# A gather loop on GpSimd written out, with constant waits and its indices loaded 256 columns at a time

## The reference

```python
h = (x_flat @ W_gat).reshape(M, HEADS, NUM_EXPERTS)     # 4 heads, 4 experts
loops = jnp.arange(M); src = concat([edge_index[0], loops]); dst = concat([edge_index[1], loops])
a_src = (h * att_src).sum(-1);  a_dst = (h * att_dst).sum(-1)
e = leaky_relu(a_src[src] + a_dst[dst], negative_slope=0.2)
e_max = segment_max(e, dst);  ee = exp(e - e_max[dst])
denom = segment_sum(ee, dst);  alpha = ee / (denom[dst] + 1e-16)
agg = segment_sum(h[src] * alpha[:, :, None], dst) + b_gat
scores = layernorm(agg).mean over heads;  top-2 of 4 experts, softmax weights
out = sum over experts of gate * (gelu(x @ W1 + b1) @ W2 + b2)
```

## Time and profile before

| | us |
|---|---|
| median of 3 runs | 11243.61 |
| lowest and highest | 11234.59 and 11244.57 |
| span of the profiled execution | 11633.8 |
| POOL busy in it | 7643.2 (66%) |
| DVE busy in it | 7098.4 (61%) |
| PE busy in it | 6698.5 (58%) |
| ACT busy in it | 4807.1 (41%) |

### The profile page before, as it was taken

The page is one execution under the profiler, slowest core; times in us unless marked ns, Lnnn a source line. Parts: engine busy times, 40 slices in busy tenths (PEclk is TensorE's granted clock), DMA queues, the critical chain, the costliest instruction groups (busy, mean ns, idle before and its releaser), DMA issues. The chain is left out here.

```text
span 11633.8 us, 85668 instructions
## 1 busy us (share of the span) xinstructions
PE 6698.5 (58%) x21383; PEld 2861.9 (25%) x21383; DVE 7098.4 (61%) x5424; ACT 4807.1 (41%) x5351; POOL 7643.2 (66%) x4827
## 2 busy tenths in 40 slices
PE   0178888888888888888859699700000000000569
PEld 0133333333333333333323233300000000000432
DVE  8689999999999999999953377611111111111334
ACT  0066666666666666666623277511111111110124
POOL 0089999999999999999963300076666666665027
PEclk8599999999999999999988699855555555555569
DMA  0166666666666676666640000032222222220012
GB/s 9 31 158 180 179 178 178 177 178 181 176 179 178 177 180 174 180 179 179 177 109 1 9 1 1 3 37 16 17 16 17 16 17 16 17 16 9 3 52 89
DMA packets 422049, 1072.84 MB, mean 92 GB/s; under 512 B 130450, under 2 KB 165906, under 8 KB 419554
## 3 DMA queue, kind: packets, MB, share of 16 engines
q1 hardware_dynamic: 336898, 1043.89, 34.4%
q0 software_dynamic: 75808, 26.27, 5.2%
q10 hardware_dynamic: 9216, 1.05, 0.1%
HBM read 1005.93 MB, written 63.50 MB: 92 GB/s over the span
## 5 line engine op out<-in xcount | busy, mean ns | idle before, releaser
L535 POOL TENSOR_TENSOR hC<-h,Cb 128x1024 f32<-128x1024 f32 x1536 | 3601.4, 2358 | 434.1 <-DVE h L630 410.6
L630 DVE TENSOR_TENSOR_SCAN h<-dA,B_ps 128x1024 f32<-128x1024 f32 x1344 | 3073.2, 2287 | 156.4
L308 PE MATMUL y_ps<-hC,con 128*128 128x512 f32 x6144 | 2965.9, 605 | 81.9 <-DVE gz L636 80.3
L2583 POOL DMA_INDIRECT g_got<-scratch_node,g_idx x2048 | 1946.2, 950 | 904.2 <-issue 904.0
L455 ACT ACTIVATE dA<-delta,negA 128x1024 f32<-128x1024 f32 x1344 | 1535.1, 1145 | 1202.1 <-DVE h L630 1200.2
L616 DVE TENSOR_TENSOR B_ps<-dx,B_ps 128x1024 f32<-128x1024 f32 x1344 | 1623.1, 1208 | 166.2 <-PE B_ps L302 166.2
L2599 PE MATMUL g_ps_y<-g_wout,g_hid 128*128 128x64 f32 x512 | 125.8, 427 | 2546.2 <-issue 1541.7
L308 PEld LDWEIGHTS y_ps<-hC,con 128*128 128x128 f32 x6144 | 1184.2, 193 | 1145.4 <-issue 940.9
L2669 DVE TENSOR_TENSOR g_e<-g_tgt,g_got 128x128 f32<-128x128 f32 x64 | 27.1, 424 | 2059.5 <-DMA g_got<-scratch_node,g_idx 2059.5
L302 PE MATMUL B_ps<-Bpart,sel 96*128 96x512 bf16 x2688 | 827.6, 390 | 651.1 <-DVE h L630 649.0
L2623 ACT ACTIVATE g_w_ps<-g_w 128x128 f32<-128x128 f32 x64 | 18.0, 281 | 2238.8 <-DVE g_m L2677 935.3
(11 more groups left out here) (475 smaller groups left out, 10879.8 us busy)
## 6 DMA issues: line engine op xcount, KB each, us to landing
Cb<-scratch_c_rows SPq DMA_DIRECT2D x3072, 256.0 KB, 4.0
drive<-scratch_c_rows SPq DMA_DIRECT2D x384, 256.0 KB, 5.1
g_got<-scratch_node,g_idx POOLq DMA_INDIRECT x2048
eb_share<-scratch_gate_rows SPq DMA_DIRECT2D x128, 256.0 KB, 3.5
scratch_c_rows<-BCrow SPq DMA_DIRECT2D x96, 256.0 KB, 4.0
scratch_edge<-g_out SPq DMA_DIRECT2D x64, 384.0 KB
par<-in_ssm SPq DMA_DIRECT2D x48, 395.5 KB, 5.1
scratch_place<-s_zero SPq DMA_DIRECT2D x4, 1024.0 KB, 10.6
```

The costliest lines, as they stand in the source:

```text
L308: last = nc.tensor.matmul(y_ps[:, hs], con[:, K_ID:K_ID + P], hC[k % DEEP][:, hs], start=(k == 0), stop=(k == STEPS - 1))
L535: G.tensor_tensor(hC[k % DEEP][:, :], hst[k % DEEP][:, :], Cb[k % DEEP][:, :], ALU.mult).then_inc(prod_ready, 1)
L630: V.tensor_tensor_scan(hst[k % DEEP][:, ::step], decayed[:, ::step], driven[:, ::step], 0.0, ALU.mult, ALU.add).then_inc(scanned, 1)
L2583: nc.gpsimd.indirect_dma_start(out=got[k][:, j, :], out_offset=None, in_=node_tbl, in_offset=Off(ap=idx[k][:, j:j + 1], axis=0)).then_inc( ...
```

## The change

POOL's loop is replaced by a program written out over all 64 chunks. The addition on `gate` and the semaphore `opened` go. At the head of each chunk POOL waits on `consumed` against a constant, and at every eighth chunk on the load of the indices. The index tiles become two tiles of 256 columns, each for eight chunks (`SPELL`); SP loads them, two ahead of everything else and the other six between its stores, and SP's loop over pairs is written out as well. ACT's wait on `consumed` and its index load go.

```diff
-            gate, spare = sb("gate", [P, GOTS + 1]), sb("spare", [P, 4])
-            idx = [sb(f"idx{k}", [P, CHUNK], i32) for k in range(GOTS)]
+            spare = sb("spare", [P, 4])
+            SPELL = 8
+            idx = [sb(f"idx{k}", [P, SPELL * CHUNK], i32) for k in range(2)]
...
 (SP)
-                    for k in range(GOTS):
-                        sp.dma_start(idx[k][:, :], x["src"][:, k * CHUNK:(k + 1) * CHUNK]).then_inc(idx_here[k], 16)
+                    def load_idx(b):
+                        sp.dma_start(idx[b % 2][:, :], x["src"][:, b * SPELL * CHUNK:(b + 1) * SPELL * CHUNK]).then_inc(idx_here[b % 2], 16)
+
+                    for b in range(2):
+                        load_idx(b)
...
-                    with sp.Fori(0, CHUNKS // 2) as pair:
-                        for k in range(2):
-                            c = pair * 2 + k
-                            sp.wait_ge(copied_out, c * 2 + 4)
-                            sp.dma_start(edge_v[:, bass.ds(c * (CHUNK * ROW_O), CHUNK * ROW_O)],
-                                         out[k][:, :, :].rearrange("p c f -> p (c f)")).then_inc(written[k], 16)
+                    for c in range(CHUNKS):
+                        sp.wait_ge(copied_out, c * 2 + 4)
+                        sp.dma_start(edge_v[:, c * (CHUNK * ROW_O):(c + 1) * (CHUNK * ROW_O)],
+                                     out[c % 2][:, :, :].rearrange("p c f -> p (c f)")).then_inc(written[c % 2], 16)
+                        if c % SPELL == SPELL - 1 and c // SPELL + 2 < CHUNKS // SPELL:
+                            sp.wait_ge(consumed, c + GOTS + 1)
+                            load_idx(c // SPELL + 2)
...
 (POOL)
-                    nc.gpsimd.memset(gate[:, :], 0.0).then_inc(opened, 1)
-                    with pool.Fori(0, CHUNKS // GOTS) as lap:
-                        for k in range(GOTS):
-                            pool.wait_ge(opened, lap * GOTS + k + 1)
-                            pool.wait_ge(idx_here[k], lap * 16 + 16)
-                            nc.gpsimd.tensor_tensor(gate[:, k:k + 1], gate[:, GOTS:GOTS + 1], gate[:, GOTS:GOTS + 1], ALU.add).then_inc(opened, 1)
-                            for j in range(CHUNK):
-                                nc.gpsimd.indirect_dma_start(out=got[k][:, j, :], out_offset=None, in_=node_tbl,
-                                                             in_offset=Off(ap=idx[k][:, j:j + 1], axis=0)).then_inc(gathered[k], 16)
+                    for c in range(CHUNKS):
+                        g, b, at = c % GOTS, c // SPELL, c % SPELL * CHUNK
+                        if c % SPELL == 0:
+                            pool.wait_ge(idx_here[b % 2], b // 2 * 16 + 16)
+                        pool.wait_ge(consumed, c + 1)
+                        for j in range(CHUNK):
+                            nc.gpsimd.indirect_dma_start(out=got[g][:, j, :], out_offset=None, in_=node_tbl,
+                                                         in_offset=Off(ap=idx[b % 2][:, at + j:at + j + 1], axis=0)).then_inc(gathered[g], 16)
...
 (ACT)
-                            act.wait_ge(consumed, c + GOTS + 1)
-                            nc.scalar.dma_start(idx[g][:, :], x["src"][:, bass.ds(((c + GOTS) % CHUNKS) * CHUNK, CHUNK)]
-                                                ).then_inc(idx_here[g], 16)
```

More of the change, by code:

```diff
@@ L2531, in graph_stage @@
             R = two_banks[:, 0:ROWS * (CHUNK + 1)].rearrange("p (f c) -> p f c", f=ROWS)
-            loaded, opened, link = sem("loaded"), sem("opened"), sem("link")
-            gathered, idx_here = ([sem(f"{n}{k}") for k in range(GOTS)] for n in ("gathered", "idx_here"))
+            loaded, link = sem("loaded"), sem("link")
+            gathered, idx_here = [sem(f"gathered{k}") for k in range(GOTS)], [sem(f"idx_here{k}") for k in range(2)]
             consumed, exps, written = sem("consumed"), sem("exps"), [sem("written0"), sem("written1")]
@@ L2569, in _ @@
                     for k in range(2):
                         sp.wait_ge(written[k], 16 * (CHUNKS // 2) + 16)
-                    for k in range(GOTS):
-                        sp.wait_ge(idx_here[k], 16 * (CHUNKS // GOTS) + 16)
                 @block.gpsimd
                 def _(pool):
-                    nc.gpsimd.memset(gate[:, :], 0.0).then_inc(opened, 1)
-                    with pool.Fori(0, CHUNKS // GOTS) as lap:
-                        for k in range(GOTS):
-                            pool.wait_ge(opened, lap * GOTS + k + 1)
-                            pool.wait_ge(idx_here[k], lap * 16 + 16)
-                            nc.gpsimd.tensor_tensor(gate[:, k:k + 1], gate[:, GOTS:GOTS + 1], gate[:, GOTS:GOTS + 1], ALU.add).then_inc(opened, 1)
-                            for j in range(CHUNK):
-                                nc.gpsimd.indirect_dma_start(out=got[k][:, j, :], out_offset=None, in_=node_tbl,
-                                                             in_offset=Off(ap=idx[k][:, j:j + 1], axis=0)).then_inc(gathered[k], 16)
+                    for c in range(CHUNKS):
[6 more added lines that the diff above has]
+                                                         in_offset=Off(ap=idx[b % 2][:, at + j:at + j + 1], axis=0)).then_inc(gathered[g], 16)
```

## The result

The changed kernel takes 11264.24 us, median of 20 runs (11245.84 to 11277.09), and the kernel before 11231.70 us, median of 20 runs (11219.25 to 11253.43). The ratio is 1.0025 with a 95% interval of 1.0018 to 1.0032: slower by about 28 us (20 to 36); the two medians lie 32.5 us apart. The forecast was 249 us faster.

What follows compares the result with a forecast made beforehand. GpSimd (POOL), issuing the indirect gathers, was taken as the bound. Savings of 300.2 us, plus 20.3 for the late start and 31 for supply, gave -248.9 us: 11243.6 to 10995 us, range 10940 to 11275.

Steps and rivals of the forecast that it cites:

- the slow pace: Gaps between POOL's L2583 gathers grow from 0.30 to 0.454 us after about 7880; blamed on the loop's later laps.
- The term of 279.9 us: POOL's loop written out with constant waits: gather gaps become 0.305 us, idle 904.2 falls to 624.3, saving 279.9 us.
- rival 2: Slow gather pace is in the profiled execution alone, so only the late start remains: 11261 us; chance 0.08.
- Nothing ties them to this stage: Argument against rival 2: the profiled span's 390.2 us above the median need not lie in the gather stage.
- the late start: POOL's first gather waits for VectorE's memset of X: +20.3 us net at the stage's start.
- no other stretch: Claim that no other POOL stretch issuing gathers or scatters without a loop is slow, citing L2479 and L2838/L2841.
- The gate operation: L2581, 64 operations at chunk heads: removal saves 20.3 us, low end 3 us.
- The new wait on `consumed`: At stage start POOL waits for VectorE's memset; scans hit gathers 0 to 3: +20.3 us, bounds +12 and +24.7.
- Indices in blocks: ScalarE's index loads go and SyncE loads blocks between stores, eight chunks ahead: 0 us.
- Supply of the written-out program: Instruction supply for written-out POOL gathers: gaps at the rate of 2.96 us per 192 transfers, +31 us, bounds 0 and 47.
- my guess: The 3.26 us gap among the L2838/L2841 transfers is a crossing between instruction blocks.
- Rival 4: Instruction shortage slows written-out gathers in all chunks: +91 us, 11335 us, up to 11450; chance 0.11.

Runs made afterwards that it cites:

- second execution: The kernel before, no edit, profiled once more: 11232.36 us, span 11230.2 us, gathers' idle time 614.4 us.
- odd execution: The profiled execution of the kernel before that the prediction read, also called first execution: span 11633.8 us, gathers' idle time 904.2 us.
- narrow tiles: The changed kernel with four index tiles of 32 columns, loaded by SP for the chunk four ahead: 11264.26 us, ratio 1.0030.

## Why the prediction was wrong

The step that failed is the first, "So I take the slow pace to belong to the loop's later laps". The rows were read rightly: 0.30 us gaps up to 7883 and 0.454 later. What they were taken for was wrong. The loop at full pace to its end in the second execution, and the same pace with the loop written out, show that it had nothing to do with laps. The term of 279.9 us was therefore nothing. It was rival 2, at 0.08, that named it, for the reason that the span stood 390.2 us above the timed median. That argument was stronger than I made it: the two later profiles have spans 1.8 and 2.2 us under their own times (11263.0 and 11264.76 for the changed kernel, 11230.2 and 11232.36 for the one before). "Nothing ties them to this stage" was no argument against, when the slow gaps came to some 290 of the 390 us. That rival 2's 11261 us lies 3 us from the measured 11264.24 is luck: it was counted from 11243.6, where the kernel before now has 11231.70, and its +17 us hold only the late start and not the longer gathers. The range holds the result only because it was stretched over the rivals; that says nothing for the forecast. I also counted a coincidence as evidence: there was one loop and one onset. And "no other stretch" was incomplete: L2333 is written out too, 128 more gathers, in the same execution at gaps of 0.31 us at most behind the first wait.

The other terms, one by one:

- *The gate operation*: forecast 20.3 us saved, low end 3. Its 11.5 us of idle time, but for the first index wait and about 1 us, were part of the odd execution (0.9 for 57 in the second). 64 operations of 0.206 us with a gap of 0.15 behind them replace gaps of 0.305, about 0.05 each: the low end.
- *The new wait on `consumed`*: forecast +20.3, between 12 and 24.7. Measured 17.6 in the traces; 15.7 when taken away, and 19.1 by the trace (about 15 by the timed runs) when added alone. Its mechanism was right in each part: the memset on X releases POOL (28.90 us), four gathers take some 4 us each, 17 places are lost. The targets landed 3.8 us sooner than before (29.0 us behind L2483, not 32.8), where 0.9 was forecast: 21.2 less 3.8 are the 17.4 that the sum should have had.
- *Indices in blocks*: 0, and 0 by the narrow tiles (sum +27.7 against +27.4).
- *Supply of the written-out program*: forecast +31. Measured none. The gap of 3.26 us in the earlier trace rows belongs to its own stage: it is there again in the second execution (3.16) and in the changed kernel (3.33), in all twelve traces before the 114th of those 128 gathers, while 2048 gathers, written out, have none. It was no rate to carry over. The traces speak against my guess that it was a crossing to a new block of instructions: the gap keeps its place while the last fetch ahead of it lies 27 us earlier in one trace and 79 in another. Its cause stays open. By the Trainium skill (Runtime: NRT & Kernel Launch, "Instruction fetch mechanics") the crossings of straight code are mostly hidden. The trace agrees: in 7600 to 10156 us the changed kernel fetched 15 blocks of 8192 bytes of instructions, one for about every 128 gathers, as this line of the view of DMA queues shows (packets, MB, share), and no gap between gathers exceeds 0.31 us.

```profile
q14 instruction: 15, 0.12, 0.0%
```

- *What was missing*: the gathers' own duration, 944 to 952 ns, 14.3 us in 2048, less some 4.5 us for the gates and the rounding of gaps. It was held constant without a bound; taking the gate operation away was priced as a saving alone, and it cost the 8 ns a gather.
- *Rival 4's price* was also added up wrong: it kept the 20.3 us of the late start and left out the 20.3 saved with the gates, which the sentence behind it cancels (+71, not +91), and a gap in each of 64 chunks comes to 11457 so, not 11450. Nothing of the result hangs on it.

The Trainium skill (SBUF — State Buffer, "SBUF: two separate sides") says that VectorE in a two-port mode or with two SBUF inputs can keep GpSimd from the port that they share, and so from writing descriptors. The trace agrees beside the long scans (4.06 to 4.41 us a gather). In the chunks the rule has no part: in the changed kernel the gathers beside VectorE's short operations last 951 to 952 ns on average and those beside none 951.

Late start 17.6 and longer gathers 9.8 are the 27.4 us. What stays open: why the first execution ran so, why this addition makes gathers shorter, and what in a build moves all gathers by 3 ns.

## What to carry to other kernels

Before a gain is priced from a profile, hold its span against the timed runs: where they differ by more than the effect, the difference has to be placed first, and a pace that changes in mid-loop is where to look for it. A wait moved from an index load to a "buffer free" semaphore also inherits everything ahead of that semaphore's first increment; for the first lap, whose buffers are free, it can be left out. After taking out a small operation, compare the durations of the ones around it, not only the gaps, and use the same instruction in a stage that no edit touches as the measure: it tells an effect of the edit from one of the build.

## What the runs showed of the hardware

- An indirect gather of 128 rows of 80 bytes took GpSimd 952 ns (median) in the four kernels that ran no 128x1 addition just before the gathers, and 944 or 947 ns in the eight traces of those that did, whether at each chunk or once. Against the gathers of L2333 in the same trace it is 8 ns each time.
- Not every addition does it. In the second execution of the kernel before, a 128x1 addition (L523) runs at 5967.81 us, and the first 64 gathers of L2333 are at 944 ns; then come copies and additions of 128x1024 and two memsets, and the second 64 are at 952. All traces have this step of 8 ns. Which of these operations brings it back to the longer time no run shows.
- It lasts into the next stages. The 128 gathers of L2838 and L2841 are at 996 ns in the kernel before and at 1003 and 1004 in the changed one:

```profile
L2840 POOL DMA_INDIRECT j_far<-scratch_carry,carry_idx x64 | 64.3, 1004 | 22.5 <-issue 22.5
```

- Two builds with the same program on GpSimd, which differ only in the order of six loads on SyncE, had all these gathers 3 ns apart (947 against 944, 955 against 952).
- Beside a scan over 2048 fp32 columns on VectorE (4.48 us) a gather took 4.06 to 4.41 us in the changed kernel; beside the short VectorE operations of a chunk (0.16 to 1.53 us) it took on average what it took beside nothing (951 to 952 ns against 951 in the changed kernel).
- One execution in the set had, from its sixth chunk on, many gathers whose starts lie 1.40, 2.10, 2.80 or 3.50 us apart instead of 1.25. None of the eleven later profiles shows this.
